# Graph network kernel on one core: a constant row loaded on another queue, the bias rows and two key comparisons moved on VectorE

## What is computed

```python
src = jnp.concatenate([_s, _d, _loop]); dst = jnp.concatenate([_d, _s, _loop])   # 8704 edges
bias = jnp.full((n, n), NEG); bias = bias.at[diag, diag].set(0.0)
bias = bias.at[dst, src].set(edge_weight)        # layer 0: additive mask of the attention
scores = jnp.einsum('hnd,hmd->hnm', q, k) / np.sqrt(HEAD_DIM) + bias
...
agg = jax.ops.segment_sum(msg, dst, num_segments=n)   # layers 1 and 2, four edge types in layer 2
```

## Time and profile before

| what | us |
|---|---|
| median of 3 runs | 529.7 (529.44 to 530.45) |
| the profiled execution's own time | 532.03 |
| its span, first to last instruction | 530.1 |
| PE busy in the span | 503.2 (95%) |
| DVE busy | 382.8 (72%) |
| ACT busy | 225.7 (43%) |
| POOL busy | 277.7 (52%) |
| mean granted TensorE clock | 0.992 |

### The profile page before, as it was taken

How to read it: one execution, slowest core, us unless ns; L and a number is a source line. 1 busy time by engine, 2 the same in 40 slices (tenths; PEclk the granted TensorE clock), 3 DMA queues, 4 the chain that set the end, 5 groups by cost and what they waited for, 6 DMA issues and landing times.

```text
span 530.1 us, 7860 instructions
## 1 busy us (share of the span) xinstructions
PE 503.2 (95%) x2483; PEld 344.5 (65%) x2498; DVE 382.8 (72%) x972; ACT 225.7 (43%) x474; POOL 277.7 (52%) x283
## 2 busy tenths in 40 slices
PE   7999999999999899999999999999999999899992
PEld 2444444444786564787788888889888786565771
DVE  5999979999986776977654863764348625776586
ACT  2102370004614776557461244435535225776365
POOL 5877777777403989402552544523532752867101
PEclk9999999999999999999999999999999998999998
DMA  6923410000293441050853564322453853100002
GB/s 192 354 74 108 113 28 1 0 0 2 85 355 100 133 122 61 4 176 19 246 155 104 183 187 137 124 80 80 131 172 97 254 163 88 52 0 1 2 0 79
DMA packets 32409, 56.48 MB, mean 107 GB/s; under 512 B 5152, under 2 KB 8686, under 8 KB 31864
## 3 DMA queue, kind: packets, MB, share of 16 engines
q1 hardware_dynamic: 19276, 31.35, 19.1%
q0 software_dynamic: 11728, 18.92, 12.0%
q10 hardware_dynamic: 1372, 5.81, 3.0%
HBM read 51.79 MB, written 4.26 MB: 106 GB/s over the span
## 4 chain that ended last, share of the span: by engine, by line
PE 70%; POOL 9%; DVE 7%; issue 6%; DMA 5%; ACT 4%; POOLq 0%; DVEq 0%; ACTq 0%
PE bank L563 12%; PE bank L564 12%; PE bank L565 12%; PE bank L586 11%; PE bank L692 4%; PE bank L783 3%; PE bank L782 3%; POOL wl L389 3%; PE bank L679 3%; DMA edge_bias<-nbias 3%; POOL sp L403 2%; PE bank L670 2%; PE bank L644 2%; POOL edge_bias L444 1%; DVE sp L1479 1%
## 5 line engine op out<-in xcount | busy, mean ns | idle before, releaser
L389 POOL TENSOR_TENSOR wl<-wraw,wh 128x512 fp32r<-128x512 f32 (+1 forms) x78 | 102.1, 1324 | 71.6 <-DMA wh<-w 15.5
L586 PE MATMUL bank<-hot 128*128 128x512 bf16 x514 | 114.3, 379 | 4.3 <-DVE hot L1303 3.4
L586 PEld LDWEIGHTS bank<-hot 128*128 128x128 bf16 x528 | 51.2, 98 | 67.5 <-DVE hot L1303 6.4
L444 POOL DMA_INDIRECT edge_bias<-ew,cell_at x68 | 71.1, 1046 | 30.3 <-issue 17.7
L563 PE MATMUL bank<-wh,tl 128*128 128x512 f32 x176 | 69.5, 395 | 0.1
L565 PE MATMUL bank<-wh,th 128*128 128x512 f32 x176 | 68.8, 391 | 0.0
L564 PE MATMUL bank<-wl,th 128*128 128x512 f32 x176 | 68.7, 390 | 0.0
L1303 DVE TENSOR_SCALAR hot<-iota,pair_dst,digit 128x1024 bf16<-128x1024 f16 x68 | 41.9, 616 | 0.2 <-issue 0.2
L955 ACT ACTIVATE sp<-sp,peak 128x512 f32<-128x512 f32 x44 | 31.8, 723 | 23.6 <-DVE peak L1479 23.2
L1302 DVE TENSOR_SCALAR hot<-iota,ef 128x512 bf16<-128x512 f16 x68 | 37.7, 554 | 4.9 <-PE bank L586 3.9
L1284 DVE SCALAR_TENSOR_TENSOR eq<-keyb,key,later 128x384 f16<-128x384 f16 (+1 forms) x68 | 40.1, 612 | 0.0
(11 more groups left out here) (239 smaller groups left out, 1062.1 us busy)
## 6 DMA issues: line engine op xcount, KB each, us to landing
wraw<-w SPq DMA_DIRECT2D x26, 256.0 KB
wh<-w POOLq DMA_DIRECT2D x6, 1024.0 KB, 6.3
keyb<-edge_keys ACTq DMA_DIRECT2D x4, 1088.0 KB, 9.7
wh<-w_rel POOLq DMA_DIRECT2D x4, 1024.0 KB, 5.9
wraw<-w_rel SPq DMA_DIRECT2D x16, 256.0 KB
wraw<-w_qkv SPq DMA_DIRECT2D x8, 256.0 KB
wh<-w_o POOLq DMA_DIRECT2D x2, 1024.0 KB, 6.8
count_rows<-counts SPq DMA_DIRECT2D x1, 2048.0 KB, 14.1
```

The costliest lines, as they stand in the source:

```text
L389: pool.tensor_tensor(wl[n % WSLOTS][:, k, 0:width], wraw[:, q % 3, 0:width], wh[n % WSLOTS][:, k, 0:width], ALU.subtract).then_inc(s["w_lo ...
L444: pool.indirect_dma_start(out=bias_dram, out_offset=bass.IndirectOffsetOnAxis(ap=cell_at[:, c:c + 1], axis=0), in_=ew[:, c:c + 1], in_offs ...
L586: mm = pe.matmul(ps(name)[:], hot[:, slot, 0, i * P:(i + 1) * P], hot[:, slot, 1 + kind, :], start=False, stop=last, skip_group_check=True)
```

## The change

It does three things:

- The load of `iota` is issued by SP, ahead of all its other loads, and no longer by ACT.
- `second` and `bias_rows` are made behind the first sweep's loop, ahead of the first chunk that is built for the second sweep, and no longer between c9 and c11.
- Of the four marks with two settles behind the bank copies, two marks and one settle now stand behind the second of the three chunks that are built ahead of the copies. The other two marks and the other settle stay.

```diff
@@ sync
             eng = sp_
+            eng.dma_start(iota[:], iota_d.to_broadcast([P, 2 * N])).then_inc(s["ld_iota"], 16)
             eng.dma_start(ei[:], edges.rearrange("a p c -> p a c")).then_inc(s["ld_edge"], 16)
@@ scalar
-            act.dma_start(iota[:], iota_d.to_broadcast([P, 2 * N])).then_inc(s["ld_iota"], 16)
             act.wait_ge(s["row_keys"], 1)
@@ vector
                 build_chunk(FIRST_PLACED * RING + slot, slot)
-                if slot == 1:
-                    dve.wait_ge(s["ld_ident"], 16)
-                    link(dve.tensor_reduce(second[:], ident[:, 1::32], AX_X, ALU.add))
-                    link(dve.tensor_scalar(second[:], second[:], -1.0, None, ALU.mult))
-                if slot == 2:
-                    dve.wait_ge(s["ld_bias"], 64)
-                    bias_rows(rows[:], slice(0, P), 0)
@@
             before, behind = CBLOCKS[0] * RING, (CBLOCKS[0] - FIRST_PLACED) * RING
+            dve.wait_ge(s["ld_ident"], 16)
+            link(dve.tensor_reduce(second[:], ident[:, 1::32], AX_X, ALU.add))
+            link(dve.tensor_scalar(second[:], second[:], -1.0, None, ALU.mult))
+            dve.wait_ge(s["ld_bias"], 64)
+            bias_rows(rows[:], slice(0, P), 0)
             dve.wait_ge(ld_keys[2], 16)
             dve.wait_ge(ld_keys[3], 16)
             for slot in range(RING - 1):
                 dve.wait_ge(s["hot_used1"], before - RING + slot + 1)
                 build_chunk(before + slot, slot)
+                if slot == 1:
+                    mark(behind, 0)
+                    mark(behind, 1)
+                    settle(behind, behind // GROUP, 0)
             for i in range(T):
                 wait_full(dve, ("counts", 0, 4 + i))
                 frees(dve.tensor_copy(packed[:, 4 + i, :], ps(("counts", 0, 4 + i))[:]), ("counts", 0, 4 + i))
             build_chunk(before + RING - 1, RING - 1)
-            for k in range(GROUP):
-                mark(behind, k)
-                if k % 2:
-                    settle(behind, behind // GROUP, k // 2)
+            mark(behind, 2)
+            mark(behind, 3)
+            settle(behind, behind // GROUP, 1)
```

## The result

The changed kernel is slower: a median of 531.83 us (530.51 to 534.49, 9 runs) against 530.08 (529.44 to 530.45, 9 runs), ratio 1.0042, 95% interval 1.0024 to 1.0060. Timed again later it was 532.48 against 529.59, ratio 1.0054 (1.0035 to 1.0074). That is 1.75 and 2.9 us, where the forecast was no change. The kernel before, timed against itself as a control, gave 0.9994 (0.9982 to 1.0007). Two single executions in the later experiments, at 848.3 us (e1) and 574.9 us (e7), lie far from all others and are left out everywhere. The profiled execution of the changed kernel took 534.49 us, with a span of 532.6.

What follows compares the result with a forecast made beforehand. PE, busy for 95% of the span, was taken to bound the kernel. The terms 0.2 - 0.67 + 1.02 - 1.03 = -0.48 us gave 531.6 from 532.03, and 529.2 for the runs' median, range 528.2 to 530.8.

Steps and rivals of the forecast that it cites:

- load of iota: Kernel start: issuing iota ahead of ei on SP's queue costs +0.2 us, bounds -0.2 and +0.6.
- border: Between the sweeps: bank copies end 0.35 us later and PE's 0.67 is given back, +1.02 us; bounds 0 and +1.93.
- break at 29.46: First sweep: without the bias rows c12 is built 1.58 us earlier, so PE's break goes, -0.67 us.
- DVE would come at 58.80: End of first loop: DVE reaches c32's build 1.58 us before 60.38, if the ring lets it.
- the ring: First loop's chunk slots: c32 may be built when c28 is used, at 58.8, or 58.1 with the break gone.
- The break at 81.34: Second sweep, c8: DVE's 3.31 us hole keeps its place in the program, PE's whole break goes, -1.03 us.
- the hole doesn't follow: Rival, before c8: the hole ends at a fixed moment, 529.7 us, or is an accident, 530.3; chance 0.25.
- second end: Before c8: the hole is an accident of the profiled execution, timed runs never had the break; +0.55 us, 530.3.
- other end: Before c8: the hole ends at a fixed moment, c8 comes at 81.34 as before; 529.7 us.
- The copies come later still: Slower rival, border: copies end 1.26 us late, term +1.93; 530.1 us with the hole, 531.2 without; chance 0.22.
- two reasons: First loop: POOL holds DVE about once in a block, and the ring holds a DVE that is ahead.
- Both breaks go: Faster rival: DVE leaves the loop up to 1.5 us earlier, copies wait for banks; -1.5 us, 528.2; chance 0.18.

Runs made afterwards that it cites:

- e1: Only the load of iota moved to the head of SP's queue, on the kernel before; ratio 0.9993 (0.9977 to 1.0009).
- e7: The kernel before with POOL's weight subtractions moved beside other chunks, so that none falls near 58 or 66 us; ratio 1.0049 (1.0032 to 1.0066).
- e10: The kernel before, nothing edited, a third profile; single execution, no ratio, first product at 130.24 us.
- e5: The changed kernel once more, nothing edited; 532.48 against 529.59 us for the kernel before, ratio 1.0054 (1.0035 to 1.0074).
- e9: The kernel before once more, nothing edited, timed against itself as a control; ratio 0.9994 (0.9982 to 1.0007).
- e11: The changed kernel, nothing edited, a third profile; single execution, no ratio, first product at 130.10 us.
- e6: The changed kernel with POOL's weight subtractions moved beside other chunks, none near 58 or 66 us; ratio to the kernel before 1.0013 (1.0000 to 1.0027).
- e4: The changed kernel with the load of iota back on ACT's queue; ratio to the kernel before 1.0031 (1.0017 to 1.0046).
- e12: The changed kernel with the other two marks and their settle also ahead of the bank copies; ratio to the kernel before 1.0116 (1.0094 to 1.0138).
- e2: Only the bias rows moved behind the first loop, on the kernel before; ratio 0.9996 (0.9980 to 1.0012).
- e3: Only two marks and a settle moved ahead of the bank copies, on the kernel before; ratio 1.0010 (0.9995 to 1.0025).

## Why the prediction was wrong

The time is 1.0 us above the range's upper end. Summed over the three profiles of each kernel, the steps measure as follows (mean of the changed minus mean of before):

| step | predicted | measured |
|---|---|---|
| load of iota, in PE's first chunk | +0.20 | 6.84 - 7.29 = -0.45 |
| first sweep beyond that, in the restart | -0.67 | 63.67 - 64.65 + 0.45 = -0.53 |
| border, restart to sweep 2 | +1.02 | 5.03 - 2.33 = +2.70 |
| sweep 2 to the product | -1.03 | 62.78 - 62.76 = +0.02 |
| sum | -0.48 | 131.48 - 129.73 = +1.75 |

The timed difference was 1.75 us in one comparison and 2.9 in the other. Each kernel's product varies by 2 to 3 us among its three profiles, so the agreement of the sums is loose. e10, with the latest full clock, carries most of the measured gain in the first sweep: without it the restarts of the kernel before are at 64.00 and 64.09, against the mean of 63.67 of the changed one.

- **The load of iota** had the wrong sign. I bounded the gain at 0.2 us by the two landings and took the issue for a cost. `ei` needs 3.3 to 3.7 us behind `iota` on one queue and 4.1 to 4.7 beside it on another, so the later issue is more than paid back. The rule of the Trainium skill that I weighed (DMA: Bandwidth & Descriptors, issuing engines are not separate queues) would have given +0.50. Here the runs differ from that rule: with one queue DVE started 0.41 us earlier in the mean.
- **The break at 29.46** goes, but only where there was one. e5 and the first profile of before had the full clock from about 6 us: the restart is 1.18 us earlier, near the 0.32 of the first chunk and the 0.67 of the break together. With a late clock (e9 against the changed kernel's first and third profiles) it is 64.09 against 64.02 and 64.18, no gain.
- **The border** is the step that failed. The sentence "DVE would come at 58.80" lets DVE keep the 1.58 us of the prologue through five blocks, on the condition that the ring of four slots lets it. It left at 60.05 to 60.41, which is only 0.24 to 0.34 us earlier than the kernel before where the clocks are alike (e5 against the first profile of before, the other two against e9). In the first profile of the changed kernel 0.83 of the 1.20 us that were lost in the loop went in two waits for PE's slots; in e5 it was 0.53 of 1.54. The rest went in instructions that took longer, mostly beside POOL's subtractions, and was not followed one by one. From the loop's end on, the working held: it has 5.1 us from there to the first copy, and with the loop's end at 60.05 to 60.41 it gives copies at 65.1 to 65.5. e5 and e11 have 64.99 and 65.37, and the profile of the changed kernel 67.12, since there the subtraction at 65.63 held the third build for 1.6 us more. That e6 leaves the loop at 58.77, where the prediction had 58.80, is luck as to the step: the 60.38 from which the prediction took 1.58 contained a hold of 1.5 us, and e6 has that hold gone and only half of the lead.
- **POOL's subtraction.** In all twelve profiles with a subtraction near 58 us an instruction of DVE ends 0.15 to 0.43 us behind it, whichever it is: line 1302 (1.83 us instead of 0.34) in the changed kernel, line 1303 (2.31 instead of 0.54) in e5. POOL hardly follows DVE's lead: without e4 and e10, the two with the latest full clock, its subtraction starts at 58.30 to 58.77 with the short prologue and at 58.48 to 58.86 with the old one. Both kernels pay this hold, 1.5 us each, and 1.8 in e5; so it took 0.33 us of lead in e5 and nothing in the other two. What it does take is slack: in e7, without it, DVE waits 0.74, 0.81 and 0.27 us ahead of the copies, 1.82 in all, where it has 0.85 in the profile of before. That is the room which the same edits found in e6. The second subtraction, near 66, costs only where the third build is not done before it.
- **The low clock** was in no case. PE's wait at the border was priced at its length alone. With 1.63 and 2.57 us of wait for the first copy, the clock was low for 3.41 us and cost 1.4 and 1.1; with 3.68 us, 6.83 (e12); with 0.66 and 0.61 (e11, e4) it stayed full. In these two the wait alone, shorter than in the other three, cost 1.6 us (e4 against e10, e11 against e9); so the loss is there without the low clock, and the clock adds to it. In timed runs a mean clock of 0.992 or less came in 15 of 16 runs of the changed kernel, in 37 of 94 of the kernel before, and in 5 of 12 of e6 (the single executions e10 and e11, both at 0.994, aside). It can't be read from them where in a run the low piece lies.
- **The break at 81.34** was worth nothing, as the rival "the hole doesn't follow" had it at its second end. The prediction named the possibility, an accident of an execution 2.3 us longer than the runs, gave it 0.25 together with its other end, and still put -1.03 into the sum. With that term at zero the same working gives +0.55, within 0.2%, so this term alone did not make the forecast of no change fail.
- **The rivals.** "The copies come later still" was the mechanism, and its trigger too: copies more than 0.9 us late without a hole. Its price was too small. It let DVE leave 0.67 us earlier, by the ring, instead of 0.24 to 0.34, and it held neither the second hold nor the clock; so it reached 531.2 and got 0.22. Of its two reasons the rows show the ring most directly, in the waits at c22 and c24. Its argument against the other held in two of three profiles: the subtraction near 58 costs DVE 1.5 us before and after, and only changes which instruction pays; in e5 it costs 1.8. The multiply-add of the bias rows, which it put beside that subtraction, came behind it (61.24) and took 0.75 us there. The Trainium skill (SBUF — State Buffer, the two separate sides) has the exclusive lock, and these traces agree: POOL's subtraction takes 1.3 us throughout, and DVE pays. "Both breaks go" fell at the same place.

What stays open: in how many timed runs the low clock follows the border, and so how the 1.75 to 2.9 us divide between it and the wait; where each part of the lead went in the loop beside the waits for PE; why the move of the subtractions costs the kernel before 0.49%; and why some runs fall to the low clock near 446 us.

## What to carry to other kernels

Work taken out of an engine's early part need not be slack later: a ring lets its filler run ahead by its slots only. Follow the lead block by block, and take off each wait for a slot; here 1.44 us at c12 were 0.52 at c25, and 0.83 of the loss were such waits. A run whose number agrees with a forecast is no proof of the step behind it: e6 agreed to 0.03 us, and only its control, e7, showed that it came from other terms. Before pricing a move across a point where the busiest engine waits for another, write down that engine's slack there (0.85 us here) and spend it once: two edits, each of which alone cost nothing that could be measured, cost 0.31% together. A break read in one execution is a candidate and not a term: one more profile of the unchanged kernel would have taken -1.03 out of the sum.

## What the runs showed of the hardware

- The full clock comes at 5.10 to 6.29 us in five profiles and at 10.04 to 13.65 in nine, without regard to the kernel (the kernel before: 6.29, 10.22, 13.65). The Trainium skill (TensorE: Matmul & The Clock Gate, the part on the HAM clock gate) says that the start of the full rate varies from run to run of one kernel, by 500 ns either way. The traces agree that it varies, and not on how much: 8.55 us lie between the earliest and the latest. With the latest clock the restart is late too: 65.86 in e10 against 64.09 in e9, of which 0.49 is the later first chunk.
- Near 446 us six profiles have another low piece, of 3.41 us (before, e2, e6) or 6.83 us (e3, e4, e7). Their last part, from the feed-forward products to the end, takes 146.7 to 147.5 us, and without it 145.8 to 146.2. It is in four of the five profiles with an early full clock and in two of the nine with a late one.
- A load of 102 KB issued 0.44 us later, on the same queue behind one of 256 KB, was there 0.41 us earlier than on a queue of its own (means of seven profiles each).
- An instruction of DVE beside POOL's subtraction of 1.3 us near 58 is held 1.5 to 1.8 us longer than it takes elsewhere, in all twelve profiles that have one there. By the records it began 0.37 to 0.74 us before the subtraction (POOL's recorded times are rough).
